# Self-attention inside a fused transformer block: the exponentials of four key tiles summed by accumulating transfers, and the products on the accumulators regrouped

## The reference

```
q, k, v = jnp.split(h @ qkv_w + qkv_b, 3, axis=-1)
scores = jnp.einsum('bqhd,bkhd->bhqk', qh, kh) / jnp.sqrt(d)     # d = 32
attn = jax.nn.softmax(scores, axis=-1)
out = jnp.einsum('bhqk,bkhd->bqhd', attn, vh)
```

## Time and profile before

| | us |
|---|---|
| median of 3 runs | 4026.27 |
| lowest and highest | 4024.15, 4030.8 |
| the profiled execution's own time | 4030.51 |
| its span, first to last instruction | 4028.6 |
| self-attention, its first to its last matmul | about 899 to 2681 on the span's clock |

### The profile page before, as it was taken

How to read it: one execution, slowest core, us unless ns; L and a number is a source line. 1 busy time by engine, 2 the same in 40 slices (tenths; PEclk the granted TensorE clock), 3 DMA queues, 4 the chain that set the end, 5 groups by cost and what they waited for, 6 DMA issues and landing times. The chain is left out here.

```text
span 4028.6 us, 51433 instructions
## 1 busy us (share of the span) xinstructions
PE 3706.3 (92%) x19340; PEld 2429.4 (60%) x19340; DVE 2262.3 (56%) x3958; ACT 1864.6 (46%) x3439; POOL 2218.0 (55%) x979
## 2 busy tenths in 40 slices
PE   4699979979999999999999999968999859999998
PEld 2577758854555554454555555426777737888887
DVE  2466642228777777777777777714766634222222
ACT  1456551113666666666666666644556421111111
POOL 0356540004888888888888889874677542000000
PEclk8788889987999999999999999987999869999999
DMA  7655657673031312102131311034576651111110
GB/s 226 148 155 158 167 159 225 222 191 66 18 65 27 69 27 51 45 20 62 27 69 27 68 27 30 17 89 105 147 178 172 152 199 42 42 42 42 42 42 31
DMA packets 213509, 371.42 MB, mean 92 GB/s; under 512 B 36103, under 2 KB 52999, under 8 KB 209703
## 3 DMA queue, kind: packets, MB, share of 16 engines
q1 hardware_dynamic: 213287, 368.49, 33.9%
HBM read 215.54 MB, written 144.51 MB: 89 GB/s over the span
## 5 line engine op out<-in xcount | busy, mean ns | idle before, releaser
L1995 DVE TENSOR_REDUCE a_peak<-a_sm 128x1 f32<-128x512 f32 x2048 | 1262.0, 681 | 423.0 <-PE a_sm L1819 423.0
L2060 POOL TENSOR_TENSOR a_esum<-a_esum,a_e 128x2048 f32<-128x2048 f32 x288 | 1319.8, 4583 | 101.8 <-ACT a_e L1951 86.6
L1951 ACT ACTIVATE a_e<-a_st 128x512 f32<-128x512 f32 x2048 | 1063.5, 602 | 569.3 <-PE a_st L1841 467.1
L1819 PE MATMUL a_sm<-a_k,a_q 96*128 96x512 f32 x2048 | 875.5, 435 | 28.1 <-DMA a_k<-s_k 28.1
L1841 PE MATMUL a_st<-a_q,a_k 128*128 128x512 f32 x2048 | 825.4, 405 | 6.5 <-ACT a_e L1951 4.5
L1819 PEld LDWEIGHTS a_sm<-a_k,a_q 96*128 96x128 f32 x2048 | 393.9, 192 | 481.2 <-DVE a_peak L1995 270.9
L1854 PE MATMUL a_acc<-a_e,a_v 128*32 128x512 f32 x4096 | 515.7, 598 | 0.0
L1841 PEld LDWEIGHTS a_st<-a_q,a_k 128*128 128x128 f32 x2048 | 387.6, 190 | 115.0 <-ACT a_e L1951 41.9
L2191 PE MATMUL mlp_ph<-mlp_us,mlp_w_hi 128*128 128x512 f32 x1024 | 336.8, 391 | 32.9 <-DVE mlp_raw_lo L2240 32.9
L2233 ACT ACTIVATE mlp_gelu<-mlp_ph,mlp_b 128x512 f32<-128x512 f32 x128 | 88.1, 688 | 595.1 <-PE mlp_ph L2191 595.0
L2271 POOL TENSOR_TENSOR mlp_x<-mlp_x,mlp_brow 128x2048 f32<-128x2048 f32 x8 | 37.0, 4620 | 569.6 <-DMA mlp_x<-s_x 569.3
(11 more groups left out here) (151 smaller groups left out, 5174.1 us busy)
## 6 DMA issues: line engine op xcount, KB each, us to landing
p_qs<-s_q SPq DMA_DIRECT2D x192, 256.0 KB, 5.9
s_q<-p_qo SPq DMA_DIRECT2D x64, 512.0 KB, 7.6
a_q<-s_q SPq DMA_DIRECT2D x96, 256.0 KB, 5.1
a_k<-s_k SPq DMA_DIRECT2D x24, 1024.0 KB, 15.8
s_x<-p_x SPq DMA_DIRECT2D x16, 1024.0 KB, 4.3
s_u<-p_ut_hi SPq DMA_DIRECT2D x64, 256.0 KB, 5.9
s_u<-p_ut_lo SPq DMA_DIRECT2D x64, 256.0 KB, 6.4
p_us<-s_u SPq DMA_DIRECT2D x16, 1024.0 KB, 7.8
```

Of the source, the lines that this page charges most:

```text
L1819: mm = pe.matmul(sm[:, bank_of_unit(j, u), x * KE:(x + 1) * KE], q[0:3 * DH, j % QR, h, qt * P:(qt + 1) * P], k[0:3 * DH, g % 2, h, kc * K ...
L1951: act.activation(e[0:KR, (j * NKT + kt) % ER, h], st[0:KR, place(kt, h) % RING], ACT.Exp, scale=SCALE).then_inc(score_read, 1)
L1995: dve.tensor_reduce(dst, src, AX.X, ALU.max).then_inc(unit_read, 1)
L2060: pool.tensor_tensor(esum[:], e[:, slot(0)] if x == 1 else esum[:], e[:, slot(x)], ALU.add).then_inc(e_added, 1)
```

## The change

In lists and rings:

- `POOLED` goes from 11 tiles to 10, so POOL makes 9 adds in a step and not 10.
- `SUMMED` goes from 5 tiles to 2.
- A new list `MOVED` holds 4 tiles. POOL issues a transfer of each from `e` into a new buffer `esum_moved` (128x2048): the first one copies, the other three add to what is there (`accum_op`). Each waits for the one before. PE multiplies the result with ones in one product, `add_moved`.
- A step thus has 16 + 2 + 1 + 1 = 20 products, in 11 blocks behind positions 0, 5, 10, 16, 22, 27, 33, 39, 44, 53 and 59. The one at 44 holds three, those at 22, 33 and 53 hold one, the others two.
- `HEAD` goes from 14 to 21 and `TURN` from 60 to 49.
- `e` has 5 slots and not 4; the ring of q has 3 and not 4; `sums` has one buffer and not two; `den_t` shares its memory with `inv_b`.

```diff
-    QR = 4
-    ER = 4
-    POOLED = [0, 1, 2, 4, 6, 7, 9, 11, 12, 13, 14]
-    SUMMED = [3, 5, 8, 10, 15]
+    QR = 3
+    ER = 5
+    POOLED = [0, 1, 3, 5, 7, 8, 9, 11, 13, 14]
+    MOVED = [2, 6, 10, 12]
+    SUMMED = [4, 15]
-    TURN = 60
-    HEAD = 14 if NKT > 1 else U
+    TURN = 49
+    HEAD = 21
-    DIVIDE_AT = (16, 24, 52)
-    FETCH_AT, SPREAD_AT = 9, 37
+    DIVIDE_AT = (13, 23, 57)
+    FETCH_AT, SPREAD_AT = 10, 42
...
+            def add_moved(i, j):
+                pe.wait_ge(e_moved, DMA * (BODY * i + j + 1) * len(MOVED))
+                for h in range(GH):
+                    mm = pe.matmul(acc[h * DH:(h + 1) * DH, 1], ones[0:KR], esum_moved[:, h], start=False, stop=False, tile_position=(0, h * DH))
...
-                elif x == 9 and exists(i, j - 1):
+                elif x == 10 and exists(i, j - 1):
+                    add_moved(i, j - 1)
                     add_partial(i, j - 1)
-                    weigh(i, j - 1, 15)
...
-                    before = (kt - ER) % NKT
-                    if before in POOLED and (kt >= ER or exists(i, j - 1)):
-                        act.wait_ge(e_added, (n - (kt < ER)) * ADDS + max(POOLED.index(before), 1))
+                    before, m = (kt - ER) % NKT, n - (kt < ER)
+                    if m >= 0 and before in POOLED:
+                        act.wait_ge(e_added, m * ADDS + max(POOLED.index(before), 1))
+                    if m >= 0 and before in MOVED:
+                        act.wait_ge(e_moved, DMA * (m * len(MOVED) + MOVED.index(before) + 1))
...
+            def move(i, j, y):
+                n, kt = BODY * i + j, MOVED[y]
+                pool.wait_ge(score_read, number(i, j, place(kt, GH - 1)) + 3)
+                if y == 0:
+                    pool.wait_ge(tile_used, n * NKT + ER)
+                    pool.dma_start(esum_moved[:], e[:, (j * NKT + kt) % ER]).then_inc(e_moved, DMA)
+                else:
+                    pool.wait_ge(e_moved, DMA * (n * len(MOVED) + y))
+                    pool.dma_start(esum_moved[:], e[:, (j * NKT + kt) % ER], accum_op=ALU.add).then_inc(e_moved, DMA)
             def step(i, j):
                 for x in range(1, len(POOLED)):
+                    if x == 1 and exists(i, j):
+                        move(i, j, 0)
+                    if x == 3 and exists(i, j):
+                        move(i, j, 1)
+                    if x == 6 and exists(i, j):
+                        move(i, j, 2)
+                    if x == 8 and exists(i, j):
+                        move(i, j, 3)
                     if x == 9 and exists(i, j - LATE):
                         scale(i, j - LATE)
-                    if x == 8 and exists(i, j + 1):
+                    if x == 6 and exists(i, j + 1):
                         lower_parts(i, j + 1)
```

More of the change, by code:

```diff
@@ L1671, in attention @@
         rows = sb("rows", [P, 2, W])
-        sums = sb("sums", [P, 2, 2, W])
-        den_t = sb("den_t", [P, W])
+        sums = sb("sums", [P, 2, W])
         inv = sb("inv", [P, W // DH])
         inv_b = sb("inv_b", [P, W])
+        den_t = inv_b
         inv_t = sb("inv_t", [P, 2, W])
@@ L1855, in weigh @@
                                    start=(kt == 0), stop=(kt == NKT - 1), tile_position=(0, h * DH))
-                if kt in POOLED or kt in SUMMED_FIRST:
+                if (kt in POOLED or kt in MOVED or kt in SUMMED_FIRST) and kt < NKT - 1:
                     mm.then_inc(tile_used, 1)
@@ L1863, in add_up @@
                     mm = pe.matmul(acc[h * DH:(h + 1) * DH, 1], ones[0:KR], e[0:KR, (j * NKT + kt) % ER, h], start=(kt == SUMMED[0]),
-                                   stop=False, tile_position=(0, h * DH))
-                if kt not in SUMMED_FIRST:
+                                   stop=(False), tile_position=(0, h * DH))
+                if kt not in SUMMED_FIRST and kt < NKT - 1:
                     mm.then_inc(tile_used, 1)
@@ L1877, in products @@
                     add_up(i, j - 1, 15)
+                elif x == 5 and exists(i, j - 1):
                     weigh(i, j - 1, 14)
-                elif x == 9 and exists(i, j - 1):
+                    weigh(i, j - 1, 15)
+                elif x == 10 and exists(i, j - 1):
+                    add_moved(i, j - 1)
                     add_partial(i, j - 1)
-                    weigh(i, j - 1, 15)
-                elif x == 14 and exists(i, j):
+                elif x == 16 and exists(i, j):
                     weigh(i, j, 0)
-                elif x == 20 and exists(i, j):
@@ L1885, in products @@
                     weigh(i, j, 1)
+                elif x == 22 and exists(i, j):
                     weigh(i, j, 2)
+                elif x == 27 and exists(i, j):
                     weigh(i, j, 3)
-                elif x == 25 and exists(i, j):
-                    add_up(i, j, 3)
-                elif x == 30 and exists(i, j):
+                    add_up(i, j, 4)
+                elif x == 33 and exists(i, j):
                     weigh(i, j, 4)
-                    add_up(i, j, 5)
+                elif x == 39 and exists(i, j):
@@ L1905, in products @@
                     weigh(i, j, 10)
+                elif x == 59 and exists(i, j):
                     weigh(i, j, 11)
-                elif x == 63 and exists(i, j):
                     weigh(i, j, 12)
-                    weigh(i, j, 13)
             def step(i, j):
@@ L1963, in fetch_sums @@
                 act.wait_ge(tile_used, (n + 1) * NKT + ER)
-                act.wait_ge(scaled, n + 1)
-                act.activation(sums[:, j % 2], acc[:], ACT.Copy).then_inc(acc_read, 1)
+                act.wait_ge(scaled, n + 2)
+                act.activation(sums[:], acc[:], ACT.Copy).then_inc(acc_read, 1)
             def step(i, j):
@@ L2012, in divide @@
                     dve.wait_ge(acc_read, n + 2)
-                    ins = dve.transpose(den_t[:], sums[:, j % 2, 1])
+                    if n > 0:
+                        dve.wait_ge(divided, DIVIDES * n)
+                    ins = dve.transpose(den_t[:], sums[:, 1])
                 else:
```

19 lines of the change are left out of this document (9 added, 10 removed).

## The result

| us | before | after |
|---|---|---|
| median, first comparison (4 runs each) | 4028.53 | 3997.47 |
| lowest and highest | 4024.15, 4034.73 | 3991.66, 4006.39 |
| median, second comparison (11 and 6 runs) | 4024.54 | 4002.69 |
| the profiled execution's own time | 4030.51 | 4006.39 |
| its span | 4028.6 | 4004.6 |

The changed kernel is faster: the ratio is 0.9933 (0.9917 to 0.9949), and in the second comparison 0.9940 (0.9927 to 0.9953). That is 22 to 31 us. The forecast was 56, with 3970; the direction and the mechanism held, and the gain was about half of it or less.

A forecast was written before the change was run, and what follows sets the result against it. PE was taken as the bound: its list of 51.3 us plus 0.6 of stalls gave a 51.9 us step against 54.0. Over 32 steps -67, with +4 and +7, made -56: 4026.3 to 3970 us, range 3950 to 4060.

The forecast's parts named there:

- PE bound, and the prices: Self-attention step: PE's own list sets it; a pair costs 0.47 us, a block of one, two or three products 1.19, 2.04, 2.99.
- 51.3: PE's list for one changed step without stalls, in us: 30.08 for pairs, 20.84 for blocks, 0.36 for turning the peaks.
- That adds some 0.15, so I take 0.6 to 0.65 of stalls: PE's stalls a step, in us: five stretches of six pairs and one of nine add 0.15 to the earlier 0.5.
- The waits of 0.04: In PE's longer stretches, the unit k = 5 (counted from 0) waits 0.04 us for a bank DVE is reading.
- First add 13.7 after position 0: Sign in the later profile: POOL's first add of a step starts about 13.7 us after score position 0.
- POOL becomes the bound: Rival: POOL's loop, 46.0 + 4d us for issue time d, sets the step if d is over 1.5; chance 0.20.
- the change gives PE nothing: Rival: PE's removed products stood beside stalls that return; step stays 54.0 less at most 0.3, total 4030 us; chance 0.11.
- The landing: Accumulating 1 MB transfers take 8.6 us from issue to landing, fitting by 1.3; rival of late landing, slower, chance 0.14.
- the 9.9 that they had: Longest landing time, in us, for the fourth transfer before ACT's wait for its slot holds up PE.
- Just behind the fourth transfer; I take 1 us of wait each, +7.: Seven group starts load 4 MB of k and v there; 1 us of wait each (0 to 3), +7 in all.
- The prologue: Before step 0: seven more units at DVE's 0.60 us each, with no score matmul beside them, +4.2 us.
- The last step but one: PE needs only 47 us there, but POOL's loop holds it at 50.4; before it was 53.1.

The follow-up runs named there:

- e8_no_transfers: Changed kernel without its transfers: PE sums the four moved tiles with one product each, in the same 11 blocks, `add_moved` left out; 4054.16 us, step 55.28.
- e9_no_moved_product: Changed kernel whose transfers run but whose moved sum is not multiplied (`add_moved` call removed, denominators lack four tiles); 3981.71 us, step 51.88.
- e1_ring: Changed kernel with a score matmul's bank chosen by running number, so three banks stay over the border of two steps; 3990.56 us, ratio 0.9912, step 52.31.
- e2_half_peaks: Changed kernel with DVE taking each maximum over 256 of 512 columns, a probe only; 3968.06 us, step 52.02.
- e12_ring_half: Changed kernel with both three banks over the border of two steps and maxima over half the columns; 3972.32 us, step 51.59.
- e3_second_later: Changed kernel with POOL's second transfer of a step issued behind its third add, not its second; 3988.91 us, ratio 0.9908, step 52.73.

## Why the prediction was right, and where it was wrong

**PE bound, and the prices: right.** "51.3" without stalls is what the cycles give, to 0.1; e8_no_transfers and e9_no_moved_product show 0.85 a product over whole steps, and that POOL and the transfers don't hold an ordinary step.

**"That adds some 0.15, so I take 0.6 to 0.65 of stalls": the term that was mis-sized.** It is 1.45: 0.65 in the five stretches of six, 0.43 at the border, 0.32 in the stretch of nine and some 0.05 elsewhere. The waits of 0.04 were right, but their price was not: the matmul behind such a wait takes 0.50 and the next one starts 0.10 later than else, so that five stretches lose 0.65 and not 0.2. And the border's 0.43 was not in it at all: I read the new place of the blocks, but not that `near` leaves two banks at the border, and that the block behind position 63 had covered it. e1_ring, e2_half_peaks and e12_ring_half show both sizes. So a step gained 1.27 and not 2.1: 29 intervals gave 37 and the last two 4, some 41 in all and not 67. That is most of what is missing.

**POOL: right, with more room.** "First add 13.7 after position 0": position 0 stands at 1312.51 - 52.73 = 1259.78, the first add at 1273.39, so 13.6. An ordinary step on POOL, answering to the earlier trace rows:

```profile
1230.91 0.88 POOL L2094 DMA_DIRECT2D a_esum_moved<-a_e  x1 [0.92 <-ACT a_e L1959]
1231.54 14.35 POOL L2070 TENSOR_TENSOR a_esum<-a_esum,a_e 128x2048 f32<-128x2048 f32 x3
...
1246.44 0.51 POOL L2077 TENSOR_TENSOR a_neg<-a_minus,a_neg 128x16 f32<-128x16 f32 x1
...
1256.17 0.87 POOL L2094 DMA_DIRECT2D a_esum_moved<-a_e  x1
1256.77 4.86 POOL L2070 TENSOR_TENSOR a_esum<-a_esum,a_e 128x2048 f32<-128x2048 f32 x1
1261.32 1.55 POOL L2083 TENSOR_TENSOR a_o<-a_sums,a_inv_t 128x512 f32<-128x512 f32 x1
1262.56 4.85 POOL L2070 TENSOR_TENSOR a_esum<-a_esum,a_e 128x2048 f32<-128x2048 f32 x1
```

```profile
1269.87 1.04 PE L1875 MATMUL a_acc<-a_esum,a_ones 128*32 128x512 f32 x8
```

An issue takes 0.6 (the copy) or 0.87 (an accumulation: the next add starts 0.6 later and is 0.26 longer), against the 1.1 that I took. The last add ends at 1267.41, and PE asks at 1269.87: 2.5 of slack for the forecast 1.3. At the peaks it is 1.4 (1246.95 against 1301.06 - 52.73 = 1248.33), forecast 1.0. The rival "POOL becomes the bound" is out, and so is "the change gives PE nothing".

**The landing: right.** All transfers by line, and who waited for them (us in sum, times):

```profile
L2091 POOL DMA_DIRECT2D a_esum_moved<-a_e x32: 583/594/765, 954.0 to 2600.9; - x32
...
  POOL a_esum_moved L2094: 25.7, 6
...
DMA to landing us min/median/max: 4.4/4.7/14.3
```

```profile
L2094 POOL DMA_DIRECT2D a_esum_moved<-a_e x96: 828/872/899, 965.7 to 2635.8; - x96
...
DMA to landing us min/median/max: 6.9/7.5/9.7
```

Accumulating transfers land in 6.9 to 9.7, under the 9.9 that they had; I took 8.6. The fourth one never made PE stand in an ordinary step. In the very last step, which has no next one behind it, PE stood 2.83 for its landing and 2.44 for POOL's last add (at 2642.84 and 2647.01), partly at half the clock; that step still took less than in before, 49.9 against 51.5.

**The group starts: right place, wrong transfer.** "Just behind the fourth transfer; I take 1 us of wait each, +7." It was the first transfer, the plain copy, that was caught among the loads (up to 14.3), and what made it dear was the second, which stood at the head of POOL's program behind it: the six waits of 25.7 us in the rows above. By the prediction's own times the second is issued 23.15 - 12.6 = 10.5 after the first (10.9 in the trace), and the 13.2 to 14.3 that the first takes beside the loads were never laid beside that. Nor have all seven starts loads, but six. Over before, which had 0.4 at these places itself, it cost 13; e3_second_later shows that 9 of it hang on the second transfer's place.

**The prologue: right.** +4.2 forecast, +4.3 measured.

**The last step but one: right number, and not by POOL.** It took 50.6, forecast 50.4 because POOL's loop would hold it. But PE's waits there name ACT (0.57 at 2588.76), and e8_no_transfers, where POOL makes no transfers, has 53.15 with three products more: 53.15 - 3 x 0.85 = 50.6 again. So the number came out by luck, as far as these rows go; what did hold that step was not tried.

**The sum.** -41 for the steps, -1 for a single interval of 55.3 that only before had, +13, +4: -25, where the profiled pair shows -25.2 for the self-attention.

## What to carry to other kernels

On a PE that is full, price a wait not by its length but by the restart behind it: here 0.03 us of waiting cost 0.13, and a block placed where a ring was short had been worth 0.43. When a program order is regrouped, look at what the moved piece had covered at its old place. When a transfer waits on another from an engine that has work behind it, lay the whole traffic of the rarest phase (here the loads of a new group) beside it, and keep one more operation between the two; one line did that here and gave back 9 us.

## What the runs showed of the hardware

An accumulating transfer of 1 MB within SBUF landed in 7.5 us (median), a plain copy of the same size in 4.7. The Trainium skill says that an add in the transfer path reads two sources and so runs at half the copy's rate (Collectives: The Full Stack, The bandwidth ceiling: the fold count and why AG ≠ RS ≠ AR). By the fit in DMA: Bandwidth & Descriptors (Anatomy of one DMA) I estimate 4.4 for the copy and 6.8 for the accumulation; the trace agrees in the order and is 0.3 and 0.7 above.

A plain copy beside 4 MB of loads took 13.2 to 14.3 us in six starts of after, while the accumulations, all issued later in a step, stayed within 9.7. The other way round the transfers slow the loads: three issues of q on SP took 2.75 us in after (median; the row below has 2.91), and 1.34 in before. In e8_no_transfers it is 1.26, so it is the transfers that do it.

```profile
1206.70 2.91 SPq L1745 DMA_DIRECT2D a_q<-s_q  x3
```

No PE row of an ordinary step waits for q. Why an issue on SP takes longer beside transfers from GpSimd was not tried.

PE at a granted clock of 1.00, made to stand, fell to 0.50 in some cases and not in others: behind a stand of 1.59 us in e1_ring it fell, for 3.4 us, and behind one of 2.55 in e12_ring_half it did not. At 0.50 a score matmul took 0.63 to 0.79 us, where it takes 0.40 to 0.50 else. So a stand can cost more than its length on a PE that is full, and the same edit that shortens a step can bring such stands about.
